# CIN recommendation tower on one core: two of seven K tiles contracted natively in the first eight chunks, first loads reordered, two copies moved to ScalarE

## The reference

```
e  = stack of tbl_f[ids[:, f]] for f = 0..38            # (B, 39, 16)
x0 = e
x1[b,h,d] = sum over i,j of W0[h, i*39+j] * e[b,i,d] * e[b,j,d]     # h = 0..127
x2[b,h,d] = sum over i,j of W1[h, i*39+j] * x1[b,i,d] * e[b,j,d]
z  = concat(x1 summed over d, x2 summed over d, dense_ctx)          # 128 + 128 + 16
y  = relu(relu(z @ W_top1 + b1) @ W_top2 + b2) @ W_top3
```

## Time and profile before

| what | us |
|---|---|
| median of 3 runs | 784.18 (783.13 to 784.47) |
| the profiled execution | 780.78 |
| its span, first to last instruction | 779.0 |
| TensorE busy with matmuls | 696.8 (89%) |
| VectorE busy | 674.9 (87%) |
| GpSimd busy | 501.0 (64%) |
| ScalarE busy | 420.2 (54%) |
| transfers of SP's queue, share of 16 DMA engines | 60.3% |

### The profile page before, as it was taken

The page is one execution under the profiler, slowest core; times in us unless marked ns, Lnnn a source line. Parts: engine busy times, 40 slices in busy tenths (PEclk is TensorE's granted clock), DMA queues, the critical chain, the costliest instruction groups (busy, mean ns, idle before and its releaser), DMA issues.

```text
span 779.0 us, 17028 instructions
## 1 busy us (share of the span) xinstructions
PE 696.8 (89%) x6210; PEld 595.1 (76%) x6210; DVE 674.9 (87%) x864; ACT 420.2 (54%) x769; POOL 501.0 (64%) x406
## 2 busy tenths in 40 slices
PE   0222678999999999999999999999999999999997
PEld 0222455878888888888888888888888888888887
DVE  5653999999999999999999999999999999888810
ACT  0001465656566656557565656655566656575741
POOL 6777887878787877868787887888787850000000
PEclk9999899999999999999999999999999999999999
DMA  4369569696867777787869796777867695854000
GB/s 101 90 156 275 129 184 164 164 171 170 163 167 168 131 185 130 187 134 190 161 163 168 173 162 169 171 148 182 141 171 142 162 160 138 162 153 133 13 7 1
DMA packets 171030, 115.67 MB, mean 148 GB/s; under 512 B 135043, under 2 KB 146906, under 8 KB 170563
## 3 DMA queue, kind: packets, MB, share of 16 engines
q1 hardware_dynamic: 154750, 108.80, 60.3%
q0 software_dynamic: 12800, 3.30, 6.6%
q10 hardware_dynamic: 3397, 2.47, 1.1%
HBM read 104.08 MB, written 15.53 MB: 154 GB/s over the span
## 4 chain that ended last, share of the span: by engine, by line
PE 77%; POOL 7%; DMA 4%; DVE 4%; issue 4%; SPq 3%; ACT 0%; DVEq 0%; ACTq 0%; POOLq 0%
PE z_ps L424 18%; PE x_ps L384 12%; PE x_ps L388 11%; PE x_ps L385 11%; PE g_ps L414 8%; POOL e_rows L360 7%; PE x1T_ps L445 4%; PE aux_ps L373 4%; PE x1T_ps L403 3%; PE x1T_ps L437 2%; SPq L280 2%; PE x1T_ps L435 2%; DVE product_lo L676 2%; DVE products L668 2%; DMA e_scratch<-e_d 2%
## 5 line engine op out<-in xcount | busy, mean ns | idle before, releaser
L360 POOL DMA_INDIRECT e_rows<-in_tbl_dram,ids_sb x400 | 500.6, 1252 | 134.7 <-issue 119.8
L514 ACT CAST product_hi<-products 117x1024 fp32r<-117x1024 f32 (+1 forms) x256 | 242.6, 948 | 102.7 <-DVE products L668 101.7
L676 DVE TENSOR_TENSOR product_lo<-products,product_hi 117x1024 fp32r<-117x1024 f32 (+1 forms) x256 | 277.4, 1084 | 23.1 <-ACT product_hi L514 22.9
L668 DVE TENSOR_TENSOR products<-bases 117x1024 f32<-117x1024 f32 (+1 forms) x256 | 277.5, 1084 | 7.1 <-DMA bases<-eT_scratch 6.5
L384 PE MATMUL x_ps<-product_hi,w_hi 117*128 117x512 f32 x448 | 198.5, 443 | 14.2 <-ACT product_hi L514 10.4
L424 PEld LDWEIGHTS z_ps<-G,w1T 128*128 128x128 f32 x1248 | 165.0, 191 | 17.3 <-issue 0.5
L385 PE MATMUL x_ps<-product_hi,w_lo 117*128 117x512 f32 x448 | 178.2, 398 | 0.0
L424 PE MATMUL z_ps<-G,w1T 128*128 128x128 f32 x1248 | 178.1, 280 | 0.0
L388 PE MATMUL x_ps<-product_lo,w_hi 117*128 117x512 f32 x448 | 148.5, 401 | 19.0 <-DVE product_lo L676 19.0
L388 PEld LDWEIGHTS x_ps<-product_lo,w_hi 117*128 117x128 f32 x448 | 84.3, 190 | 43.6 <-DVE product_lo L676 23.7
L384 PEld LDWEIGHTS x_ps<-product_hi,w_hi 117*128 117x128 f32 x448 | 85.6, 191 | 28.4 <-issue 13.8
(11 more groups left out here) (55 smaller groups left out, 340.1 us busy)
## 6 DMA issues: line engine op xcount, KB each, us to landing
bases<-eT_scratch SPq DMA_DIRECT2D x155, 468.0 KB
e_diag<-e_scratch SPq DMA_DIRECT2D x512, 10.0 KB
id_spread<-id_scratch SPq DMA_DIRECT2D x16, 437.5 KB
e_rows<-in_tbl_dram,ids_sb POOLq DMA_INDIRECT x400
e_scratch<-e_d SPq DMA_DIRECT2D x16, 320.0 KB, 9.5
eT_scratch<-e_rows SPq DMA_DIRECT2D x16, 312.0 KB
eT_scratch<-eT_scratch SPq DMA_DIRECT2D x16, 312.0 KB
w1T<-in_L_rec_W_dram SPq DMA_DIRECT2D x1, 2496.0 KB, 19.3
```

What stands on the lines that cost most here:

```text
L360: nc.gpsimd.indirect_dma_start(out=e_rows[t % E_SLOTS][:, f * D:(f + 1) * D], out_offset=None, in_=tables[f], in_offset=bass.IndirectOffse ...
L514: nc.scalar.copy(product_hi[:, first:first + count, :], products[:, first:first + count, :]).then_inc(hi_ready, 1)
L668: nc.vector.tensor_tensor(products[:, first:first + count, :], bases[u % 2][:, b:b + count, cols], bases[u % 2][:, a:a + 1, cols].to_broad ...
L676: nc.vector.tensor_tensor(product_lo[:, first:first + count, :], products[:, first:first + count, :], product_hi[:, first:first + count, : ...
```

## The change

In the first eight chunks (`EARLY = 2 * CPT`), group 1, two K tiles, is contracted natively in float32 from `products` and an unsplit copy of the weights, `w_whole`; its rounding on ScalarE and its subtraction on VectorE are left out, and the counts of `hi_ready` and `lo_ready` are adapted by `rounds`. SP issues w1T and the dense layers' weights before the first store of eT, issues the first two chunks' base loads itself, ahead of the first store of e, and waits for chunk 0's before it goes on. In the loop `double_eT` moves behind the spread of its chunk, and `store_e` of the next tile from c = 0 to c = 2. `copy_e` and the rounding of the dense context move from VectorE to ScalarE; `copy_e` of tile t+1 goes from VectorE's c = 0 to the end of ScalarE's c = 1.

```diff
+EARLY, WHOLE = 2 * CPT, 1
+WHOLE_TILES = slice(GROUPS[WHOLE][3], GROUPS[WHOLE][3] + GROUPS[WHOLE][2])
...
+def whole(g, n):
+    return g < EARLY and n == WHOLE
+def rounds(g, n):
+    left_out = min(g, EARLY) + (g < EARLY and n >= WHOLE)
+    return g * NG + n + 1 - left_out if g >= 0 else 0
...
         w0_lo = sb("w0_lo", [R, NT, H], f32r)
+        w_whole = sb("w_whole", [R, GROUPS[WHOLE][2], H])
...
+            sp.dma_start(w1T[:, :, :], w1).then_inc(w1_loaded, 16)
+            sp.dma_start(wt1_cin[:, :, :], w_top1[0:2 * H, :].rearrange("(k p) n -> p k n", p=128)).then_inc(mlp_loaded, 16)
+            sp.dma_start(wt2[:, :, :], w_top2.rearrange("(k p) n -> p k n", p=128)).then_inc(mlp_loaded, 16)
+            sp.dma_start(wt3[:, :], w_top3).then_inc(mlp_loaded, 16)
+            sp.dma_start(bias1[:, :], b_top1).then_inc(mlp_loaded, 16)
+            sp.dma_start(bias2[:, :], b_top2).then_inc(mlp_loaded, 16)
...
             store_eT(0)
-            store_e(0)
...
             sp.wait_ge(eT_doubled, 16)
-            load_base_part(sp, 0, 0, HB // 2, first_ready[0])
+            for c in range(2):
+                load_base_part(sp, 0, c * (HB // 2), HB // 2, first_ready[c])
+            store_e(0)
+            sp.wait_ge(first_ready[0], 16 * LOADS)
...
                 t, c = divmod(g, CPT)
-                if c == 1 and t + 1 < TILES:
-                    double_eT(t + 1)
...
-                if g == 0:
-                    sp.dma_start(w1T[:, :, :], w1).then_inc(w1_loaded, 16)
-                if g == 3:
-                    sp.dma_start(wt1_cin[:, :, :], w_top1[0:2 * H, :].rearrange("(k p) n -> p k n", p=128)).then_inc(mlp_loaded, 16)
-                    sp.dma_start(wt2[:, :, :], w_top2.rearrange("(k p) n -> p k n", p=128)).then_inc(mlp_loaded, 16)
-                    sp.dma_start(wt3[:, :], w_top3).then_inc(mlp_loaded, 16)
-                    sp.dma_start(bias1[:, :], b_top1).then_inc(mlp_loaded, 16)
-                    sp.dma_start(bias2[:, :], b_top2).then_inc(mlp_loaded, 16)
+                if c == 1 and t + 1 < TILES:
+                    double_eT(t + 1)
...
                     store_eT(t + 1)
+                if c == 2 and t + 1 < TILES:
                     store_e(t + 1)
...
                 _, _, count, first = GROUPS[n]
-                pe.wait_ge(hi_ready, g * NG + n + 1)
+                if whole(g, n):
+                    pe.wait_ge(product_ready, g * NG + n + 1)
+                    for k in range(first, first + count):
+                        last = nc.tensor.matmul(x1_ps[:, :], w_whole[:, k - first, :], products[:, k, :], start=False, stop=False)
+                    last.then_inc(contracted, 1)
+                    return
+                pe.wait_ge(hi_ready, rounds(g, n))
...
                     nc.tensor.matmul(x1_ps[:, :], w0_lo[:, k, :], product_hi[:, k, :], start=False, stop=False)
-                pe.wait_ge(lo_ready, g * NG + n + 1)
+                pe.wait_ge(lo_ready, rounds(g, n))
...
                     look_up(t, n)
-            pe.wait_ge(w0_split, 2)
+            pe.wait_ge(w0_split, 3)
...
             def round_products(g, n):
+                if whole(g, n):
+                    return
...
+            def copy_e(t):
+                act.wait_ge(gathered[t % E_SLOTS], (t // E_SLOTS + 1) * 16 * len(GATHERED))
+                act.wait_ge(looked_up, (t + 1) * sum(map(len, SETS)))
+                after(act, e_stored, 16 * t)
+                nc.scalar.copy(e_d[:, :, 0:F], e_rows[t % E_SLOTS][:, :].rearrange("b (f d) -> b d f", d=D)).then_inc(e_d_ready, 1)
+            def round_dense(t):
+                act.wait_ge(dense_loaded, (t + 1) * 16 * 3 * GAP // D)
+                after(act, h1_in_ps, M1 * t)
+                nc.scalar.copy(dense_parts[:, :], dense_now[:, :]).then_inc(dense_hi_ready, 1)
...
                               w0[j:j + count, 0:halves, shift, :]).then_inc(w0_loaded, 16)
-            act.wait_ge(eT_doubled, 16)
-            load_base_part(act, 0, HB // 2, HB // 2, first_ready[1])
+            copy_e(0)
             round_products(0, 0)
-            act.wait_ge(w0_split, 2)
+            act.wait_ge(w0_split, 3)
...
                     copy_z2(t - 2)
+                if c == 1 and 0 <= t - 2 < TILES - 2:
+                    round_dense(t - 2)
...
                     round_products(g + 1, 1)
+                if c == 1 and t + 1 < TILES:
+                    copy_e(t + 1)
+                if g == CHUNKS - 1:
+                    round_dense(TILES - 2)
+                if g == CHUNKS + CPT:
+                    round_dense(TILES - 1)
...
         def _(dve):
-            def copy_e(t):
-                dve.wait_ge(gathered[t % E_SLOTS], (t // E_SLOTS + 1) * 16 * len(GATHERED))
-                dve.wait_ge(looked_up, (t + 1) * sum(map(len, SETS)))
-                after(dve, e_stored, 16 * t)
-                nc.vector.tensor_copy(e_d[:, :, 0:F], e_rows[t % E_SLOTS][:, :].rearrange("b (f d) -> b d f", d=D)).then_inc(e_d_ready, 1)
...
             def split_dense(t):
-                dve.wait_ge(dense_loaded, (t + 1) * 16 * 3 * GAP // D)
-                after(dve, h1_in_ps, M1 * t)
-                nc.vector.tensor_copy(dense_parts[:, :], dense_now[:, :]).then_inc(dense_hi_ready, 1)
...
                     dve.wait_ge(bases_ready[u % 2], (u // 2 + u % 2) * 16 * LOADS)
-                after(dve, lo_ready, (g - 1) * NG + n + 1)
+                if whole(g - 1, n):
+                    after(dve, contracted, (g - 1) * NG + n + 1)
+                else:
+                    after(dve, lo_ready, rounds(g - 1, n))
...
             def lower_parts(g, n):
+                if whole(g, n):
+                    return
                 _, _, count, first = GROUPS[n]
-                dve.wait_ge(hi_ready, g * NG + n + 1)
+                dve.wait_ge(hi_ready, rounds(g, n))
...
             dve.wait_ge(w0_step, 1)
+            nc.vector.tensor_copy(w_whole[:, :, :], w0_sum[:, WHOLE_TILES, :]).then_inc(w0_split, 1)
             nc.vector.tensor_copy(w0_hi[:, :, :], w0_sum).then_inc(w0_split, 1)
-            dve.wait_ge(w0_split, 1)
+            dve.wait_ge(w0_split, 2)
...
                                     wt1_dense[2 * GAP:3 * GAP, :].bitcast(f32), ALU.subtract).then_inc(wt1_dense_split, 1)
-            copy_e(0)
...
                     pick_rows(t + 1, 3)
-                if c == 0 and t + 1 < TILES:
-                    copy_e(t + 1)
```

## The result

The changed kernel takes 777.86 us (median of five runs, 775.34 to 780.12) against 783.13 us for the kernel before in the same session: ratio 0.9934, 95% interval 0.9910 to 0.9959. It is faster, by 5.3 us where 8.2 were forecast, and inside the range. The profiled execution took 776.82 us (span 775.0), 4.0 less than the profiled one of before.

A forecast was written before the change was run, and what follows sets the result against it. VectorE bounds some eight chunks, then TensorE at 42.53 us a tile, with SP dating the data. SP 8 us sooner at tile 2, other terms about cancelling, gives 784.2 - 8.2 = 776.0 us, range 768 to 785.

The forecast's parts named there:

- The frame: SP's queue sets the date of bases and ids, deciding how much of VectorE's gain can be kept.
- The first product: VectorE's first product at 57 us, 5.5 us sooner; this gain not on the path that sets the end.
- the upper bound: First product at 66 us if the early constants hold up the gathers, w0 or eT of tile 0.
- Tile 1's bases: Rows at 75.5, eT 5.3, double 3.0, bases at most 13.8: chunk 4 starts at 97.6, 14 us sooner.
- The ids: Ids of tile 3 land at about 105 us, needed some 4 us into chunk 4.
- Tile 2: SP can store eT of tile 2 at about 113.5 us, 8 us sooner than 121.67.
- the sum: SP 8 us sooner at tile 2, smaller terms roughly cancelling, gain kept after chunk 8: 784.2 - 8.2 = 776.0.
- The landing: Tile 2's gathered rows land an estimated 2.5 us after the last gather, near 113.5 us.
- SP's tile: SP's time per tile: 16.5 us from store of eT to bases, 41.8 to 42.3 in all.
- Rival (a): SP's queue becomes the bound, its tile passing 42.53 us (43.4 if stores are held): 787.5 us; chance 0.16.
- ScalarE's copy of e: Copy of 624 columns per tile moved to ScalarE, put at about 0.75 us.
- Rival (c): Tile 1's gather lands as late as before, bases 1 clogging the engines; VectorE's time becomes waits: 783.5 us; chance 0.08.

The follow-up runs named there:

- run 3: Kernel of before with only the native contraction of the second group in the first eight chunks added: 781.28 us, ratio 0.9989.
- run 5: Kernel of before with two edits, the constants issued at the start and the native contraction in the first eight chunks: 778.17 us, ratio 0.9941.
- run 1: Changed kernel with its constants put back, w1T to chunk 0 and the tower's weights to chunk 3, each behind its spread: 784.0 us, ratio 1.0039.
- run 4: Kernel of before with only the constants moved to the start, ahead of the first stores: 782.07 us, ratio 1.0004.
- run 9: Changed kernel with the copy of e back on VectorE in each tile's first chunk: 779.18 us, ratio 0.9962.
- run 7: Changed kernel with the first store of e right behind the first store of eT again: 777.92 us, ratio 0.9929.
- runs 11 and 12: Changed kernel, first three bases on their own semaphore, one subtraction inside the wait; ids ahead of third chunk's spread (782.99 us) or only of the store of e (776.44).
- run 6: Changed kernel with the doubling of eT ahead of bases and spread again: 778.65 us, ratio 0.9974.

## Why the prediction was right, and where not

- **The frame held.** SP sets the date of the data, and that decides how much of VectorE's gain is kept: run 3 kept none of it, run 5 most. The gain is made before 200 us and stays: x1 of chunk 16 was evacuated at 248.67 for 253.71, that of chunk 63 at 742.95 for 746.95. About 1 us was lost in between.
- **The first product** was put at 57, bounds to 66; it came at 68.05. The step that failed is the upper bound: it names the constants' hold on w0 but gives it too little, as VectorE waited 11.27 us for w0. Runs 1 and 4 tie that wait to the constants: gone where they go back, 11.18 us where they alone are moved. That the first product is not on the path held for the changed kernel, where VectorE's later waits (5.24, 2.54, 2.71 us) take up what it would give; in run 4, with nearly no waits behind it, it is on VectorE's line to chunk 8. What the prediction didn't see is that SP's part of the start is on it: the chain of work that ended last goes through the first store of eT (43.72), its double, the store of e (65.16) and the spread to the store of eT of tile 1.
- **Tile 1's bases**, 97.6 forecast, let chunk 4 begin at 107.18. Two terms failed. The rows were to land 5.6 us after the last gather's issue (75.5); where VectorE or SP waits for nothing else they are awaited for 6.8 us (run 9) and 7.4 (run 7), and in the changed kernel the store went out at 78.56 (+3.1), right behind spread(0). And store to double took 11.5 us, not 5.3 (+6.2). I took the time from tile 0 of before; tile 1's in before took 5.3 too, VectorE busy throughout (79.80 to 85.13), and tile 0's in the changed kernel 9.0 (43.72 to 52.74). What makes it long no run separates. From the double to the product it was 17.2 us for 16.8.
- **The ids** of tile 3 were forecast at about 105 and arrived at 113.81, as all that stands ahead of them on SP was late.
- **Tile 2**: 8 us sooner was the forecast, 4.6 came (117.12 for 121.67). This is most of what the sum had too much (its terms give 8 us, its last line takes 8.2). The pace of the gathers was right, 25 from 71.64 to 108.06, 1.52 us each (GpSimd's timeline of the changed kernel, first fence). So the sum's 1.56 stood rightly against the rule that the prediction takes from the Trainium skill (SBUF — State Buffer, "Who interferes with whom") at its word. The landing was not: 2.5 us after the last issue, as estimated, would be 110.6. In run 5 VectorE waits for these rows until 118.00, 8.9 us after their last issue at 109.08 (its timeline, second fence). In the changed kernel two more things end just then: the pick, 116.87, which stands behind VectorE's waits for bases and ids, and SP's spread(4), 117.02. SP has no wait of any size from 93.22 to that store, so there the store waited for its turn on the queue, but only just: had SP come sooner, the pick would have held it at once. So the step that failed is that SP could store when the rows land: late from tile 1's double on, its queue wasn't free before.

```profile
71.64 0.94 POOL L376 DMA_INDIRECT e_rows<-in_tbl_dram,ids_sb  x1 [0.31 <-issue]
...
108.06 1.16 POOL L376 DMA_INDIRECT e_rows<-in_tbl_dram,ids_sb  x1 [0.30 <-issue]
```

```profile
118.00 0.69 DVE L633 COPY e_d<-e_rows 128x624 f32<-128x624 f32 x1 [3.75 <-DMA e_rows<-in_tbl_dram,ids_sb]
```

- **SP's tile**: 16.5 us to the bases forecast, 133.32 - 117.12 = 16.2 measured; 41.8 to 42.3 for the tile forecast, 158.65 - 117.12 = 41.5 measured. Rival (a), which needed more than 42.53, fell.
- **TensorE** works 699.6 - 696.8 = 2.8 us more, 3.0 forecast. **ScalarE's copy of e** takes 1.28 us, not 0.75 (row below, its timeline in the changed kernel), and no run shows that it matters.

```profile
86.78 1.28 ACT L586 COPY e_d<-e_rows 128x624 f32<-128x624 f32 x1
```

- **What the sum didn't say**: it let VectorE be up to 16 us sooner at chunk 8 and the data 8, so that VectorE had time to spare. With the first product 5.6 us later instead of 5.5 sooner there was little to spare: chunk 8 came 4.8 us sooner, after a wait of 2.71. So a second part was needed for each to count: apart, they are worth 0.1% or less; together, 0.6%. Rival (c) has run 1's mechanism, VectorE's time turned into waits (12.58 and 6.56 us), but run 1 is 0.4% slower than before and (c) was to be 0.1% faster.

## What to carry to other kernels

Where two lines reach the same point together, undoing parts one at a time misleads: each part alone is worth little or nothing here, and one of them, the native part, could be left out of the whole. Test them in pairs, one from each line. Before an operation is moved on a queue that feeds several consumers, ask for each of them what stands in front of it then: one 0.4 us issue, put ahead of a spread instead of behind it, cost 6.5 us here by the medians (runs 11 and 12).

## What was not expected

- A store of 312 KB in runs of 64 bytes has landed within 5.3 us for tiles 0 and 1 of before, and took 9.0 to 11.5 us until its double in the changed kernel's first two tiles and in run 6; the next issue on SP's queue is held in part of that time (5.81 us for one in run 7).
- The rows of a tile's last gather are there 6 to 10 us after its issue: 5.8 for tile 0 of the changed kernel, 9.9 for tile 1 of before; its 0.94 us of GpSimd tells nothing of that.
- ScalarE copies 128x624 strided words in 1.28 us, VectorE in 0.70.
- The five runs of the changed kernel order themselves by the granted clock: 775.34 and 776.82 us at 0.996, 777.86 at 0.993, 778.61 at 0.991, 780.12 at 0.989. Run 4 has no such order (780.77 us at 0.987, 783.74 at 0.996). One execution of this kernel doesn't decide a change of 0.3%.
